# One graph network kernel: the sort pass rewoven, TensorE's loop heads placed, and two orders changed in the edge networks

## The chip, the cores and the metric

One core of one Trainium2 chip runs the whole program. The metric is the time of one execution in microseconds (us), as the device takes it. Three runs of the kernel before took 17660.53, 17686.4 and 17701.15 us, so the median is 17686.4 us.

## The reference, cut to what matters

There are 12500 nodes with 16 features and 412500 edges, sorted by target. Four graph layers follow each other, each behind a layer norm and a relu, each added to the node state `x`:

```python
m = einsum('ei,ej,ijh->eh', h[dst], edge_attr, W_msg_tp) * norm
agg = segment_sum(silu(m) @ W_msg_lin, src)              # layer 0: sums by source
msg = einsum('ea,aoi,ei->eo', edge_attr, W, h[src])      # layer 1: sums by target
e = ln(mlp(edge_attr)); n = ln(mlp(h))                   # layer 2: encoders
for s in range(2):                                       # and two edge networks
    e = e + ln(mlp(concat(e, n[src], n[dst])))
    n = n + ln(mlp(concat(n, segment_sum(e, dst))))
out = gcn(relu(gcn(h, W1, b1)), W2, b2)                  # layer 3: two weighted convolutions
```

The MLPs have 64 hidden units and a silu. `mlp` and `ln` are per edge or per node.

## The kernel before, in words

The edges are cut into 104 blocks (`BLOCKS`) of 3968 edges, 128 partitions with 31 each. The first edge pass computes layer 0's messages and at the same time brings the edges of each block into an order by source ("sort pass", `sorted_message`, line 622). All later edge passes read what it stored: a convolution (`sorted_conv`), the first edge network with the edge encoder, the second edge network (both are `sorted_mlp`, line 1755, with `enc` true and false), and two gcn passes. Node passes lie between them.

Each pass is one program per engine. `in_pairs` (line 88) writes out the first six blocks and then a loop over pairs of blocks, 49 turns of two bodies each, and a few bodies that drain the pipeline. The order in `body` is the order in which an engine issues its instructions; engines meet through semaphores alone. `Chain.at("step", k)` is the count that a semaphore has when that step of block k is done.

**Sort pass.** In one body an engine works on three blocks. *Places* of block k: VectorE (DVE) turns edge ends into a cell, a one-hot matrix `hot_c` (L889), eight pieces of a one-hot matrix of targets `hot_d` (L894), then ranks (L896 to L920) and, after a matmul on TensorE (PE, L1133), the place of each edge (L923 to L944). PE counts (L1121) and turns each piece of `hot_d` (L1130) into PSUM, and ScalarE (ACT) copies it out (L1051). *Messages* of block k-1: PE multiplies each turned piece with a window of the node table (L1144), DVE multiplies the result by the edge attributes (L956, `prod`), sums it (L962) and ACT applies the silu (L1064). Then GpSimd (POOL) writes the 3968 records to their places with 31 indirect DMAs (L828), which wait for the index (L950) and for the silu. *Sums* of block k-3: SyncE (SP) loads the sorted slots back (L781), DVE makes three masked copies (L980 to L985) and four pieces of a one-hot matrix `hot` (L992), PE sums with them in float32 (L1165), ACT writes an 8-bit one-hot matrix of targets (L1082 to L1086) and the sums (L1092), POOL adds a spill (L842). In the kernel before each engine does all of places, then all of messages, then all of sums. SP issues, per body, the edge ends of k (L752 to L754), attributes, window and cleared records, the stores of k-4, and last the slots of k-2, once the 31 DMAs of that block have landed.

**Edge networks.** A block has five groups of cells. PE gathers node states by one-hot matmuls (L2404, L2411), then come a hidden layer (L2430 or L2433), an output layer `out1` (L2444), a layer norm on DVE and ACT, and the sums by target. In the first network PE also runs the edge encoder (L2349 to L2369), turns normed states (`first_` L2379, `second_` L2388), sums in float32 (L2471), and ends each body with `carry` (L2475): the carried sum of the block before and 35 matmuls of one column that count the edges. In the second network the states come from DRAM, DVE splits the normed state into three bfloat16 parts (`less0` L2034, `part2` L2038), and PE sums them (`part_sums`, L2458 and L2460).

A branch hint names the loop's back edge ahead of time. Every loop has it as the first instruction of a turn; only PE's loop of the first edge network has it between the two bodies (`hint_between`).

## Time and profile before

| | us |
|---|---|
| median of three runs | 17686.4 |
| the profiled execution | 17701.2 |
| its span, first to last instruction | 17699.5 |
| PE busy in the span | 13912.2 |
| DVE busy | 13068.0 |
| ACT busy | 7125.3 |
| POOL busy | 4621.6 |

A profile is one execution. A group of instructions is a line of the kernel, an engine and an operation with the tiles it writes and reads; "idle before" is the time in which the engine stood still just before it, with what ended that time. In a timeline a row is one instruction, or several of one line in succession (x8), with its start, its length and, in brackets, the idle time before it. "issue" is idle time in which the engine waited for nothing that the profile shows. PEclk is the granted TensorE clock as a share of 2.4 GHz. Matmuls of float32 are counted twice.

### The profile page before, as it was taken

The page shows a single profiled execution, that of the slowest core. Times are in us where ns is not written, and L with a number is a line of the kernel's source. Part 1 is how long each engine was busy: PE and PEld are TensorE (multiplying, and loading weights), DVE is VectorE, ACT ScalarE, POOL GpSimd, SP SyncE. Part 2 cuts the span into 40 slices and gives each one's busy share as a digit, 9 for nine tenths or more (in the row PEclk, how much of TensorE's full clock was granted, in tenths as well). Part 3 has the DMA queues.
Part 4 walks back from the last instruction along what each step waited for, and adds up shares of the span by engine and source line. Part 5 has one row for each costly group of instructions (what it writes and reads, how often), then busy time and mean ns, then how long its engine had stood idle before and what let it go on. Part 6 is the DMA issues. An engine that isn't in the chain of part 4 may idle for free. (4 is left out here: it accounts for less than half of the span.)

```text
span 17699.5 us, 504368 instructions
## 1 busy us (share of the span) xinstructions
PE 13912.2 (79%) x180289; PEld 12124.8 (69%) x180600; DVE 13068.0 (74%) x30392; ACT 7125.3 (40%) x15316; POOL 4621.6 (26%) x4403
## 2 busy tenths in 40 slices
PE   1677776777767997799999999996799999856565
PEld 0566666666654997588888888885577777646565
DVE  2888888888866997566656656665677777779899
ACT  0454454544542332344444444443344444411111
POOL 0677777777760110011111111110000000001111
PEclk9666666666656998899999999997899999967676
DMA  1122222222222553344444444442444444437566
GB/s 60 54 57 59 57 60 58 57 59 57 60 54 76 157 156 99 96 116 123 117 118 119 118 119 119 121 118 75 131 151 154 154 152 150 132 92 210 167 210 177
DMA packets 1347419, 1956.45 MB, mean 111 GB/s; under 512 B 705453, under 2 KB 923253, under 8 KB 1306317
## 3 DMA queue, kind: packets, MB, share of 16 engines
q1 hardware_dynamic: 1046674, 1621.50, 29.5%
q0 software_dynamic: 209664, 186.01, 7.5%
q10 hardware_dynamic: 90300, 137.10, 2.1%
q8 instruction: 666, 10.91, 0.3%
q14 instruction: 115, 0.93, 0.0%
HBM read 1443.57 MB, written 501.97 MB: 110 GB/s over the span
## 5 line engine op out<-in xcount | busy, mean ns | idle before, releaser
L828 POOL DMA_INDIRECT records<-e_sort_rec,e_sort_index x3224 | 3295.8, 1022 | 1347.4 <-issue 920.3
L2411 PEld LDWEIGHTS e_s_ps_h<-e_s_pick,e_s_parts 128*64 128x64 bf16 x61776 | 1965.7, 113 | 298.7 <-issue 137.0
L2411 PE MATMUL e_s_ps_h<-e_s_pick,e_s_parts 128*64 128x128 bf16 x61776 | 2028.9, 223 | 108.7 <-issue 108.7
L1165 PE MATMUL e_sort_acc<-e_sort_thirds,e_sort_hot 128*128 128x48 f32 x6864 | 1488.8, 414 | 301.4 <-DVE e_sort_hot L992 301.4
L1165 PEld LDWEIGHTS e_sort_acc<-e_sort_thirds,e_sort_hot 128*128 128x128 f32 x6864 | 1472.1, 332 | 332.1 <-DVE e_sort_hot L992 332.1
L2530 POOL DMA_DIRECT2D states<-e_s_second_t x520 | 480.3, 924 | 4176.9 <-ACT e_s_second_t L2259 4108.3
L2006 DVE TENSOR_SCALAR e_s_pick<-e_s_rows,lane_below 128x1024 bf16<-128x1024 bf16 (+1 forms) x3120 | 1179.1, 434 | 372.2 <-PE e_s_ps_h L2411 350.7
L2046 DVE TENSOR_TENSOR e_s_unit<-e_s_ps_o,lane_out 128x512 f32<-128x512 f32 (+1 forms) x520 | 324.9, 625 | 1421.0 <-PE e_s_ps_o L2369 1420.7
L2521 POOL DMA_INDIRECT e_s_spill<-send,e_s_lists x208 | 218.3, 1049 | 3633.1 <-PE e_s_ps_h L2433 2741.9
L1082 ACT ACTIVATE e_sort_away<-iota,e_sort_slots 128x128 f32<-128x128 f32 x3640 | 1107.5, 388 | 10.1
L2444 PE MATMUL e_s_ps_o<-w_eblk,e_s_act 128*128 128x128 f32 x7488 | 1015.1, 276 | 98.2 <-DVE e_s_unit L2055 81.6
L2444 PEld LDWEIGHTS e_s_ps_o<-w_eblk,e_s_act 128*128 128x128 f32 x7488 | 949.6, 191 | 147.9 <-DVE e_s_unit L2055 101.4
L1144 PE MATMUL e_sort_y<-e_sort_window,e_sort_turned 128*128 128x128 f32 x6448 | 988.1, 323 | 19.9 <-DVE e_sort_prod L956 19.9
L1144 PEld LDWEIGHTS e_sort_y<-e_sort_window,e_sort_turned 128*128 128x128 f32 x6448 | 942.2, 232 | 53.2 <-DVE e_sort_prod L956 30.0
L2232 ACT ACTIVATE e_s_act<-e_s_ps_h,col_eenc 128x512 f32<-128x512 f32 (+1 forms) x520 | 335.4, 645 | 1525.0 <-PE e_s_ps_h L2360 1525.0
L2471 PE MATMUL e_s_ps_sum<-e_s_unit,e_s_wide 128*128 128x128 f32 x7280 | 899.0, 275 | 0.1
L2404 PE MATMUL e_s_ps_h<-e_s_to_hot,e_s_window 128*64 128x512 bf16 (+2 forms) x6240 | 824.0, 367 | 90.9 <-DVE e_s_to_hot L2007 78.2
L1130 PE MATMUL e_sort_turn<-ident,e_sort_hot_d 128*128 128x128 bf16 x3224 | 491.6, 306 | 506.0 <-ACT e_sort_turned L1051 498.8
L1419 PE MATMUL e_s_g<-e_s_parts,e_s_pick 128*128 128x48 bf16 x20592 | 773.5, 206 | 119.8 <-DVE e_s_pick_own L1315 63.7
L2266 ACT ACTIVATE e_s_act<-e_s_ps_h,col_state 128x512 f32<-128x512 f32 (+1 forms) x1040 | 663.9, 638 | 502.5 <-PE e_s_ps_h L2430 256.2
L2471 PEld LDWEIGHTS e_s_ps_sum<-e_s_unit,e_s_wide 128*128 128x128 f32 x7280 | 854.9, 192 | 0.7 <-issue 0.7
L1419 PEld LDWEIGHTS e_s_g<-e_s_parts,e_s_pick 128*128 128x128 bf16 x20592 | 750.5, 112 | 138.1 <-issue 70.2
(558 smaller groups left out, 31254.5 us busy)
## 6 DMA issues: line engine op xcount, KB each, us to landing
e_s_rows<-rows_d SPq DMA_DIRECT2D x312, 1088.0 KB, 5.3
e_s_hot<-hots_d SPq DMA_DIRECT2D x520, 560.0 KB, 3.9
e_s_to_rows<-rows_d SPq DMA_DIRECT2D x208, 608.0 KB, 5.9
e_s_rows<-rows_d SPq DMA_DIRECT2D x208, 544.0 KB, 4.4
e_s_rows<-rows_d SPq DMA_DIRECT2D x208, 512.0 KB, 5.2
e_s_to_rows<-rows_d SPq DMA_DIRECT2D x208, 512.0 KB, 6.2
states<-e_s_first_t ACTq DMA_DIRECT2D x416, 256.0 KB, 2.1
states<-e_s_second_t POOLq DMA_DIRECT2D x416, 256.0 KB, 4.2
```

The source lines that it names most:

```text
L828: pool.indirect_dma_start(records, bass.IndirectOffsetOnAxis(ap=index[x][:, t:t + 1], axis=0), rec[x][:, t, :], None,).then_inc(written[x] ...
L1082: last = act.activation(away[:, n - c, :], iota128[:, :], ACT.Square, scale=-1.0, bias=slots[x][:, n, 1:2])
L1130: mm = pe.matmul(ps_turn[:, (n - t) * LANES:(n - t + 1) * LANES], hot_d[:, n, :], ident16[:, :], start=True, stop=True)
L1144: mm = pe.matmul(ps_y[j % 2][0:LANES, (n - t) * AF:(n - t + 1) * AF], turned[x][:, n, :], window[x][:, :], start=True, stop=True)
L1165: mm = pe.matmul(acc[sum_bank(c)][:, sum_at(c)], hot[:, c, :], thirds[:, c, :, :].rearrange("p h f -> p (h f)"), start=False, stop=last an ...
L1419: mm = pe.matmul(ps_g[g][:, at:at + 3 * F], pick[x][:, h, c * LANES:(c + 1) * LANES], parts[:, SPAN * c + h, :, :].rearrange("p r f -> p ( ...
L2006: dve.tensor_scalar(pick[p][:, h, 0:(f - c) * LANES], rows_[:, c * LANES:f * LANES], lane_below[:, h:h + 1], None, ALU.is_equal).then_inc( ...
L2266: act.activation(act1[p][:, 0:turned(s)], hidden_bank(x, s)[:, 0:turned(s)], ACT.Silu, bias=(col_state if enc else col_state1)[:, :]).then ...
L2404: pe.matmul(halves[half][:, 0:n_ * LANES], window[:, r, 1, :], to_pairs[:, half, 0:n_, :], start=r == 0, stop=False, skip_group_check=True)
L2411: mm = pe.matmul(halves[half][:, j * LANES:(j + 1) * LANES], parts[:, SPAN * c + h, r, :], pick[p][:, h, (c - c0) * LANES:(c - c0 + 1) * L ...
L2444: mm = pe.matmul(ps_o1[p % NB][:, j * LANES:(j + 1) * LANES], act1[p][:, j * LANES:(j + 1) * LANES], W[f"eblk1{rnd}"][:, :], start=enc, st ...
L2471: mm = pe.matmul(ps_sum[:, 0:2 * D if enc else D], wide[s][:, (c - c0) * LANES:(c - c0 + 1) * LANES], units_of(x, c), start=c == 0, stop=F ...
```

## The change

It has four parts.

1. Sort pass: on DVE, ACT and PE the three blocks of a body are woven together. A turn of eight pieces holds, per piece, one `hot_d` and one turn of block k, one message matmul group and one `prod` of block k-1, and pieces of DVE's sums of block k-3; the ranks and places of block k come last on DVE. ACT copies records first, and the silu stands between the second and third group of 8-bit targets. On PE the matmul that the places wait for follows the sums. The third piece of `hot` reads the constant from SBUF (`iota128`) instead of PSUM.
2. PE's loops in all passes start at the first instruction slot of a fetch block (`head_slot`), and the hint of PE's first edge network loop moves to the loop's head like all others.
3. First edge network, PE: `carry` goes ahead of the last group of `out1`.
4. Second edge network, DVE: the first picks and the windows of the next block go from the body's end to its fifth group, ahead of `less0` of the fourth group.

```diff
-def in_pairs(eng, n, delay, body, hint_between=False):
+def in_pairs(eng, n, delay, body):
...
+    at_block = {eng.engine: 0} if eng.engine == mybir.EngineType.PE else None
+    with eng.bass.Fori(3, n // 2, engines=[eng.engine], hint_back_edge=True, head_slot=at_block) as j:
+        body(j * 2, 0, 6)
+        body(j * 2 + 1, 1, 6)
...
 # sort pass, DVE
-                    if inside(k):
-                        place(k, x, before)
-                    if before >= 1 and (not isinstance(k, int) or k - 1 < BLOCKS):
-                        message(k - 1, y, before - 1)
-                    if before >= 3:
-                        sum_(k - 3, y, before - 3)
+                    if new:
+                        cells_(k, x, before)
+                    if sent:
+                        indices(k - 1, y, before - 1)
+                    for j in range(len(TURNS)):
+                        if new:
+                            target_hot(k, x, j, before)
+                        if sent:
+                            products(k - 1, y, j, before - 1)
+                        if summed_ and j == 1:
+                            thirds_low(k - 3, y, before - 3)
+                        if summed_ and j == 2:
+                            thirds_top(k - 3, y, before - 3)
+                        if summed_ and j == 3:
+                            thirds_rest(k - 3, y, before - 3)
+                        if summed_ and j in (4, 5, 6):
+                            sum_hot(k - 3, y, j - 4, before - 3)
+                    if sent:
+                        message(k - 1, y, before - 1)
+                    if summed_:
+                        sum_hot(k - 3, y, 3, before - 3)
+                        spill_rows(k - 3, y, before - 3)
+                    if new:
+                        ranks(k, x, before)
+                        places(k, x, before)
...
+                    numbers = iota128[:, :] if g in (1, 2) else ps_iota
+                    if g == 3:
+                        dve.wait_ge(bt.sem, bt.at("early", k))
...
 # sort pass, ACT
+                    if sent:
+                        message(k - 1, y, before - 1)
+                    if new:
                         place(k, x, before)
-                    if before >= 1 and (not isinstance(k, int) or k - 1 < BLOCKS):
-                        message(k - 1, y, before - 1)
-                    if before >= 3:
+                    if summed_:
                         sum_(k - 3, y, before - 3)
+                        targets(k - 3, y, 0, before - 3)
+                        targets(k - 3, y, 1, before - 3)
+                    if sent:
+                        silu_(k - 1, y, before - 1)
+                    if summed_:
+                        targets(k - 3, y, 2, before - 3)
+                        targets(k - 3, y, 3, before - 3)
+                        sums(k - 3, y, before - 3)
...
 # sort pass, PE
+                    for j in range(len(TURNS)):
+                        if sent:
+                            message(k - 1, y, j, before - 1)
+                        if new and j == 0:
+                            count(k, x, before)
+                        if new:
+                            turn(k, x, j, before)
+                    if summed_:
                         sum_(k - 3, y, before - 3, isinstance(k, int) and k == BLOCKS + 2)
+                    if new:
+                        spills(k, x, before)
+                    if summed_:
+                        sum_spills(k - 3, y, before - 3)
...
 # second edge network, DVE
+                    if inside(k) and s == NG - 1:
+                        picks(k, x, 0, before)
+                        windows(k, x, before)
                     if not enc and out_ and s >= 1:
                         less0(k - 2, x, s - 1, before - 2)
...
-                if inside(k):
-                    windows(k, x, before)
-                if inside(k):
-                    picks(k, x, 0, before)
                 if not enc and out_:
                     part2(k - 2, x, 4)
...
 # edge networks, PE
+                    if enc and out_ and s == NG + 1:
+                        carry(k - 2, x, before - 2)
                     if main and 2 <= s < NG + 2:
                         out1(k - 1, y, s - 2, before - 1)
-                if enc and out_:
-                    carry(k - 2, x, before - 2)
-
-            in_pairs(pe, BLOCKS, 2, body, hint_between=enc)
+
+            in_pairs(pe, BLOCKS, 2, body)
```

## Rows read from the trace of the kernel before

**Rows 1.** Stretches: sort pass, first edge network; engines' busy us, PEclk, DMA, GB/s

```profile
455.00:5280.00 4825.00, 3357.18 (x20994) 3027.89 (x20992) 3981.92 (x8042) 2366.87 (x6439) 3463.24 (x3328) 0.61 0.21 58
...
7265.00:12075.00 4810.00, 4573.28 (x61351) 3989.03 (x61353) 2914.53 (x7113) 2261.25 (x3917) 579.53 (x612) 0.97 0.48 119
```

The five busy times are those of PE, PE's weight loads (PEld), DVE, ACT and POOL.

**Rows 2.** Timeline of POOL, one block of the sort pass

```profile
2999.36 0.97 POOL L828 DMA_INDIRECT records<-e_sort_rec,e_sort_index  x1 [3.49 <-ACT e_sort_rec L1064]
...
3003.31 1.74 POOL L828 DMA_INDIRECT records<-e_sort_rec,e_sort_index  x1 [0.30 <-issue]
...
3040.94 1.61 POOL L842 DMA_INDIRECT agg<-e_sort_merged,e_sort_spill_at  x1 [0.30 <-issue]
3045.63 0.97 POOL L828 DMA_INDIRECT records<-e_sort_rec,e_sort_index  x1 [3.08 <-ACT e_sort_rec L1064]
```

**Rows 3.** Groups by line, 3000 to 4000 us: POOL's record writes (busy, mean ns | idle)

```profile
L828 POOL DMA_INDIRECT records<-e_sort_rec,e_sort_index x676 | 692.1, 1024 | 272.0 <-issue 192.8 <-ACT e_sort_rec L1064 72.8 <-DVE e_sort_index L950 6.4
```

**Rows 4.** Timeline of DVE, one block of the sort pass

```profile
3002.87 1.35 DVE L992 TENSOR_TENSOR e_sort_hot<-e_sort_lower,iota 128x1152 f32<-128x1152 f32 x1
...
3016.44 1.15 DVE L896 TENSOR_TENSOR e_sort_pair<-e_sort_cell 128x961 f32<-128x961 f32 x1
...
3029.51 0.19 DVE L923 TENSOR_TENSOR e_sort_spill_rank<-e_sort_within,e_sort_misc 128x31 f32<-128x31 f32 x1 [3.69 <-PE e_sort_misc L1133]
...
3031.85 0.18 DVE L950 CAST e_sort_index<-e_sort_place 128x31 int32<-128x31 f32 x1
...
3039.84 4.29 DVE L962 TENSOR_REDUCE e_sort_summed<-e_sort_prod 128x496 f32<-128x3968 f32 x1
```

**Rows 5.** Timeline of PE and ACT, sort pass: sums, messages, one target group

```profile
3003.01 14.31 PE L1165 MATMUL e_sort_acc<-e_sort_thirds,e_sort_hot 128*128 128x48 f32 x66 [2.90 <-DVE e_sort_hot L992]
...
3075.61 3.39 PE L1144 MATMUL e_sort_y<-e_sort_window,e_sort_turned 128*128 128x128 f32 x16
...
3000.43 2.73 ACT L1082 ACTIVATE e_sort_away<-iota,e_sort_slots 128x128 f32<-128x128 f32 x9
```

**Rows 6.** Timeline of SP's queue: slots of one block, edge ends after it

```profile
3042.28 0.35 SPq L781 DMA_DIRECT2D e_sort_slots<-records  x1
...
3045.55 0.39 SPq L754 DMA_DIRECT2D e_sort_first<-firsts_d  x1
```

**Rows 7.** Waits of PE, first edge network: total us, times, longest

```profile
PE e_s_ps_h L2411 <- issue: 107.0, 48, 3.5
PE e_s_ps_o L2444 <- DVE e_s_unit L2055: 80.8, 103, 0.9
PE e_s_ps_h L2349 <- issue: 42.0, 48, 1.2
```

**Rows 8.** Timeline of PE, first edge network: inside a turn, then across a turn's end

```profile
9039.92 0.60 PE L2379 MATMUL e_s_ps_u<-ident,e_s_unit 128*128 128x128 f32 x4
...
9078.74 1.02 PE L2479 MATMUL e_s_ps_sum<-ones_lane,e_s_hot 128*128 128x1 bf16 x35
...
9084.89 1.91 PE L2411 MATMUL e_s_ps_h<-e_s_pick,e_s_parts 128*64 128x128 bf16 x49 [2.44 <-issue]
...
9088.60 0.97 PE L2379 MATMUL e_s_ps_u<-ident,e_s_unit 128*128 128x128 f32 x4
```

**Rows 9.** Timeline of DVE, first edge network: the norms that these turns of state wait for

```profile
9037.33 0.69 DVE L2014 TENSOR_TENSOR e_s_unit<-e_s_unit,e_s_stat 128x512 f32<-128x512 f32 x1
...
9083.34 0.69 DVE L2014 TENSOR_TENSOR e_s_unit<-e_s_unit,e_s_stat 128x512 f32<-128x512 f32 x1 [0.42 <-DVE e_s_stat L582]
```

**Rows 10.** Waits of PE, second edge network: total us, times, longest

```profile
PE e_s_ps_sum L2458 <- DVE e_s_split L2038: 136.6, 103, 1.4
```

**Rows 11.** Timeline of DVE and ACT, second edge network: tail of a body

```profile
14050.70 0.69 DVE L2034 TENSOR_TENSOR e_s_less<-e_s_unit,e_s_split 128x512 f32<-128x512 f32 x1 [4.22 <-ACT e_s_split L2292]
...
14058.11 0.35 DVE L2038 TENSOR_TENSOR e_s_split<-e_s_less,e_s_split 128x192 bf16<-128x192 f32 x1
...
14056.95 0.35 ACT L2296 ACTIVATE e_s_split<-e_s_less 128x192 bf16<-128x192 f32 x1
```

More of the change, by code:

```diff
@@ L856, in _, with cells_ @@
             def _(dve):
-                def place(k, x, before):
+                def cells_(k, x, before):
                     src_, dst_ = srcE[x][:, :], dstE[x][:, :]
@@ L920, in place, with places @@
                     dve.tensor_reduce(within[:, :], pair[:, :, :], axis=AX.X, op=ALU.add).then_inc(av.sem, 1)
+                def places(k, x, before):
                     dve.wait_ge(av.sem, av.at("sooner_sum", k))
@@ L944, in place, with indices @@
                     dve.tensor_scalar(base_[:, :], base_[:, :], float(SLOTS), None, ALU.add).then_inc(av.sem, 1)
-                def message(k, x, before):
+                def indices(k, x, before):
                     if before >= 2:
@@ L1075, in sum_, with targets, sums @@
                     act.activation(rows_t[x][:, :], ps_rows, ACT.Copy).then_inc(bs.sem, 1)
[L1076 to L1087 removed]
+                def targets(k, x, g, before):
+                    c, e = HOTS[g]
+                    if g:
+                        act.wait_ge(bs.sem, bs.at(f"target{g - 1}", k))
+                    elif before:
+                        act.wait_ge(bs.sem, bs.end(k - 1))
+                    for n in range(c, e):
+                        last = act.activation(away[:, n - c, :], iota128[:, :], ACT.Square, scale=-1.0, bias=slots[x][:, n, 1:2])
+                    last.then_inc(bs.sem, 1)
+                    act.wait_ge(bs.sem, bs.at(f"away{g}", k))
+                    act.activation(ready_[:, :], lane[:, 0:1], ACT.Copy).then_inc(bs.sem, 1)
+                    act.activation(targets_[x][:, c * LANES // 2:e * LANES // 2].bitcast(FP8), away[:, 0:e - c, :].rearrange("p c l -> p (c l)"), ACT.Relu,
+                                   scale=-1.0, bias=1.0, saturate=False).then_inc(bs.sem, 1)
+                def sums(k, x, before):
                     act.wait_ge(bt.sem, bt.at("merged", k))
@@ L1115, in _, with count @@
             def _(pe):
-                def place(k, x, before):
+                def count(k, x, before):
                     pe.wait_ge(av.sem, av.at("hot_c", k))
@@ L1132, in place, with spills, message @@
+                def spills(k, x, before):
                     pe.wait_ge(av.sem, av.at("lates16", k))
                     pe.matmul(ps_lates, earlier16[:, :], lates16[:, :], start=True, stop=True).then_inc(at_.sem, 1)
-                def message(k, x, before):
-                    pe.wait_ge(attrs_in[x], attrs_of(k, x))
-                    pe.wait_ge(as_.sem, as_.end(k))
-                    for j, (t, e) in enumerate(TURNS):
-                        if j >= 2:
-                            pe.wait_ge(cv.sem, cv.at(f"prod{j - 2}", k))
-                        elif before:
-                            pe.wait_ge(cv.sem, cv.at(f"prod{len(TURNS) - 2 + j}", k - 1))
-                        for n in range(t, e):
-                            mm = pe.matmul(ps_y[j % 2][0:LANES, (n - t) * AF:(n - t + 1) * AF], turned[x][:, n, :], window[x][:, :],
-                                           start=True, stop=True)
-                        mm.then_inc(ct.sem, 1)
+                def message(k, x, j, before):
+                    t, e = TURNS[j]
+                    if j == 0:
+                        pe.wait_ge(attrs_in[x], attrs_of(k, x))
+                        pe.wait_ge(as_.sem, as_.end(k))
+                    if j >= 2:
+                        pe.wait_ge(cv.sem, cv.at(f"prod{j - 2}", k))
+                    elif before:
+                        pe.wait_ge(cv.sem, cv.at(f"prod{len(TURNS) - 2 + j}", k - 1))
+                    for n in range(t, e):
+                        mm = pe.matmul(ps_y[j % 2][0:LANES, (n - t) * AF:(n - t + 1) * AF], turned[x][:, n, :], window[x][:, :],
+                                       start=True, stop=True)
+                    mm.then_inc(ct.sem, 1)
```

111 lines of the change are left out of this document (45 added, 66 removed).

## The prediction, made before the changed kernel ran

> **What bounds the kernel now.** I read the busy times by stretch first, then for each changed pass the waits of the engine that is nearest to its limit, then a timeline of one block. The sort pass takes 4825 us, 46.4 us for each of 104 blocks, and no engine is full in it: DVE works 3981.92 us, 38.3 a block, PE 32.3, and PE's clock is granted at 0.61 on average [rows 1]. What turns over without a pause is POOL: the first write of a block starts at 2999.36, the spill behind the 31st ends at 3040.94 + 1.61 = 3042.55, and the next block begins at 3045.63, after 3.08 us of waiting for ACT's silu [rows 2]. So POOL's own work is 43.2 of 46.3 us. Over 1000 us the waits for the silu add up to 72.8 us, while the 192.8 us put down to "issue" are the 0.3 us between two writes and stay [rows 3]. The silu is late because DVE does all of the places first, stands still 3.69 us for a matmul queued behind PE's sums, and then only multiplies and reduces [rows 4].
>
> The first edge network is PE's: 4573 us busy of 4810, clock 0.97 [rows 1]. Its idle time has three parts, 107.0, 80.8 and 42.0 us [rows 7]. The first comes once a turn of the loop (48 times), in the first gather, 32 recorded matmuls behind the loop's head, and lasts 2.44 us in the turn shown [rows 8]. The third comes at the loop's end itself, also 48 times. The second is the last output layer waiting for DVE.
>
> In the second edge network PE waits 136.6 us, 1.33 a block, for the last `part2` of a block [rows 10]. DVE does it at 14058.11, though ACT had its input done at 14056.95 + 0.35 = 14057.30: windows and picks stand between. Earlier in the same body DVE stands still 4.22 us [rows 11].
>
> **The change, part by part.**
>
> *Sort pass, gain.* If POOL never waits for the silu, 7.28% of 4825 us goes: 351 us. Of that, one ordinary gap of 0.30 us a block stays [rows 2], 104 x 0.30 = 31 us, so 320 us is the most.
>
> *Sort pass, what is added.* The third piece of `hot` now reads its constant from SBUF, as the second does. The write that starts at 3003.31, while the SBUF piece runs (3002.87 to 4.22), takes 1.74 us, against 0.97 undisturbed: 0.77 more [rows 2, 4]. One more such meeting a block costs 104 x 0.77 = 80 us. It may miss the write's sensitive part and cost nothing, or meet two writes and cost 160; I take one meeting, as the row shows. The Trainium skill, "SBUF — State Buffer", section "Who interferes with whom", says that a DVE instruction with two SBUF inputs and a GpSimd instruction that reads SBUF exclude each other for the whole instruction, the later one blocked; that speaks against this edit, and by it the write would wait to 3004.22, 0.91 us instead of the measured 0.77, and the sum would be 95 instead of 80. Net of the sort pass: 320 - 80 = 240 us, 44.0 us a block.
>
> *Does anything else bind at 44.0?* DVE has 38.3 us of work [rows 1]. Its 3.69 us wait goes if PE's matmul for the places comes no later than the ranks. By hand, with PE at its half clock: 16 message records took 3.39 us [rows 5], so 62 take 13.1; with turns and count the eight rounds take PE about 18 us, within DVE's eight rounds, which carry the sums' pieces too. DVE's ranks and places run from 3016.44 to 3031.85, less 3.69 of waiting 11.7 us [rows 4]; they now come last, so the reduce ends at most 38.3 - 11.7 = 26.6 us into the body, some 0.7 later for the first rounds' wait. PE's sums then take 14.31 us from about 23.5 to 37.8, about when DVE's ranks are through, so that wait almost vanishes. ACT does two target groups (9 squares in 2.73 us [rows 5], about 4.1 with the rest) before the silu, which comes near 33 us; the body ends near 40.5. The bound from POOL's side: the last write of a block ends at 3040.64, SP issues the slots at 3042.28 and the last edge end at 3045.55 [rows 6], so with the landing a body can start about 7 us behind that write. POOL needs this body's silu one block and a spill later, 44.0 + 2.2 us behind the write. So the silu may come 39 us into the body: 6 us to spare. What is late next is POOL itself.
>
> *Moved steps on the queues.* SP's order is unchanged; its waits for sums and targets of k-4 are met earlier than the slots' wait, which still comes last. ACT's record copies now come ahead of its eight PSUM copies, under 2 us, while PE is still counting: nothing.
>
> *First edge network.* With `carry` (some 1.05 us, [rows 8]) ahead of the last output group, PE works where it stood: 80.8 us. With the loop's head on a block's first slot, the next block boundary lies 256 instructions away instead of a few dozen, so the following code has time to arrive: 107.0 us. The turn's end keeps perhaps half of its 42.0. That is 209 us from waits alone. Behind the stall the matmuls also run slowly (the `first_` at 9088.60 takes 0.97 us, the one at 9039.92 takes 0.60, the half and the full of 2.4 GHz [rows 8]), so more can come back. The upper bound is DVE: `first_` cannot start before the norm, which ends at 9038.02 and 9084.03, and starts 1.90 and 4.57 us later than that [rows 8, 9]; 6.47 us a turn x 49 turns = 317 us. Above that the norm's wait takes over. I take 250, nearer the waits, since the clock may still fall behind `carry`'s one-column matmuls.
>
> *Second edge network.* The moved picks and windows (2.7 us) go into the 4.22 us of standing. They need rows, lists and the last gather of the block before, all there by then. `part2` can start 14058.11 - 14057.30 = 0.8 us earlier, less 0.05 for the signal: 0.75 x 104 = 78 us; the remaining 0.57 us is ACT's.
>
> *Loop heads elsewhere.* No wait of PE in the other loops comes once a turn under "issue"; I cost them at 0, with 20 us either way for the jumps into the six loops and a worse or better boundary.
>
> **Sum.** 240 + 250 + 78 = 568 us off 17701.2 us, that is 17133. The profiled execution is 14.8 us above the median of 17686.4, so against the runs I say 17120 us.
>
> **The rivals.**
>
> *A. The stall at the fetch boundary stays* (the change doesn't do what it says: the head is not what makes it). Then the first edge network gives `carry`'s 80.8 less about 10 for the norm: 70. 240 + 70 + 78 = 388, 17298 us. For it: one row of one turn doesn't show a block's boundary. Against: the stall comes at the same place 48 times.
>
> *B. The hint at the head is spent before the turn's end*, 92 us later, and the jump pays a full fetch. Between the end of `carry` (9079.76) and the end of the stall (9084.89) lie 5.1 us [rows 8], the nearest price of a fetch. Less the 0.87 now paid, 49 x 4.2 = 207 us come back: 240 + 43 + 78 = 361, 17325 us. For it: this loop alone had its hint in the middle. Against: the second network's loop has the hint at its head, and the longest wait of PE there is the one for DVE [rows 10]. The Trainium skill, "Runtime: NRT & Kernel Launch", section "Instruction fetch mechanics", says that a taken branch to code outside the resident window must fetch before it goes on; by it B is what happens wherever the loop is longer than the window.
>
> *C. The weave is DVE's or PE's bound after all*, by stalls of some 5 us a body: POOL gets half of its waits back, the sort pass gives 120: 17238 us.
>
> *D. Slower: the eight rounds run in series.* If every round's `prod` waits for that round's message and turn on PE (1.7 + 0.45 us), 8 x 2.15 = 17.2 us come on top of DVE's 38.3: 55.5 a body, 9.2 more than now, 957 us against 328 won elsewhere: 18315 us. It decides from 49.5 us a body on. Against: the message of a round belongs to the block before, whose pieces were turned a body ago, and has two PSUM banks, so PE runs a round ahead.
>
> **How the numbers follow.** The sum as above 0.57, A 0.13, B 0.12, C 0.12, D 0.06; of C, 0.02 is a weave bad enough to leave nothing. The likeliest case's own range goes from 320 + 317 + 78 + 20 = 735 off (16951) to 160 + 209 + 60 - 20 = 409 off (17277). The range 17000 to 17400 holds A, B and C too. A measurement of this kernel tells 0.2% (35 us) from no change. Faster 0.92, same 0.02, slower 0.06.
>
> **What would show it.** Right: POOL's waits for the silu all but gone and writes following at 44 us a block; DVE's L923 waiting under 0.5 us; no PE idle above 1 us in the first network's L2411; `first_` waiting for DVE's L2014; L2458 waiting about 0.6 us. Wrong: POOL still waiting for L1064 over 1 us a block (C or D), "issue" at the loop's head above 2 us (B), or in L2411 (A).

## The result, and the profile after the change

The changed kernel takes 16981.52 us (median of 4 runs, 16973.91 to 16985.81), against 17683.37 us before (4 runs, 17660.53 to 17701.15): 0.9601 times the time before, with a 95% interval of 0.9585 to 0.9616. That is 702 us less; 563 to 566 were forecast, and 16981.5 lies 18.5 us below the range given. Line numbers from here on are the changed kernel's (or the experiment's) and differ from those of the kernel before.

Where the time went is read best by stage. The sort pass is measured from TensorE's first matmul in it to its last; each other stage from the first to the last matmul of one line of TensorE's (in the kernel before L2369 and L2433 for the two edge networks, L1710 for the convolution, L1433 for the two gcn passes):

| stage | before | after | difference | forecast |
|---|---|---|---|---|
| sort pass | 4859.9 us | 4479.0 us | -380.9 | -240 |
| first edge network | 4800.7 | 4538.8 | -261.9 | -250 |
| second edge network | 2912.8 | 2835.9 | -76.9 | -78 |
| convolution, both gcn passes | 1249.9, 1811.5 | 1250.0, 1809.7 | -1.7 | 0 |

These are the two profiled executions, which lie 727 us apart: that of the kernel before was the slowest of its four runs, that of the changed kernel the fastest. A stage of unchanged code differs by up to some 20 us between traces (the first edge network as it was takes 4779.6 us in the trace of `before_sbuf_piece`, the changed sort pass 4478 to 4494 in the seven traces that have it). With that in mind two stages came out as forecast, and the sort pass gave 141 us more. It goes first. The busy times of the two stretches in the changed kernel (columns as in [rows 1]; the stretch of the sort pass is 4444 us instead of 4825):

```profile
455.00:4899.00 4444.00, 3269.47 (x20938) 3038.85 (x20938) 3904.48 (x8040) 2340.94 (x6434) 3394.88 (x3328) 0.64 0.22 63
6884.00:11427.00 4543.00, 4456.15 (x61285) 3895.83 (x61285) 2900.95 (x7105) 2246.26 (x3907) 577.98 (x611) 1.00 0.50 125
```

POOL's own groups over the whole sort pass, record writes and spills, of the kernel before (busy, mean ns of one | idle before them and its causes):

```profile
L828 POOL DMA_INDIRECT records<-e_sort_rec,e_sort_index x3224 | 3295.8, 1022 | 1347.4 <-issue 920.3 <-ACT e_sort_rec L1064 396.6 <-DVE e_sort_index L950 29.9
L842 POOL DMA_INDIRECT agg<-e_sort_merged,e_sort_spill_at x104 | 167.4, 1610 | 55.2 <-issue 31.1 <-ACT e_sort_merged L1092 19.8 <-DMA agg<-e_sort_merged,e_sort_spill_at 4.4
```

and of the changed kernel:

```profile
L815 POOL DMA_INDIRECT records<-e_sort_rec,e_sort_index x3224 | 3220.4, 999 | 1034.6 <-issue 954.7 <-ACT e_sort_rec L1090 51.9 <-ACT e_sort_rec L1094 14.0
L829 POOL DMA_INDIRECT agg<-e_sort_merged,e_sort_spill_at x104 | 174.5, 1678 | 55.3 <-issue 31.1 <-ACT e_sort_merged L1126 19.8 <-DMA agg<-e_sort_merged,e_sort_spill_at 4.5
```

These four lines split the 381 us. POOL's idle time in front of the record writes fell by 1347.4 - 1034.6 = 313 us, where 320 were forecast. The wait for the silu went from 396.6 to 14.0; of the 396.6, 64.7 were the first block's, which now waits 51.9 for ACT's copy (L1090), and what is left in front of each block's first write, the 14.0 too, is the ordinary gap of 0.3 us. The spills cost 7 us more. And the record writes themselves became shorter, 1022 to 999 ns, which is 75 us less, where the sum had put 80 us **more** for the third piece of `hot` that now reads SBUF. So the wrong term is the collision, and it was wrong by 155 us.

The waits of DVE from 3000 to 4000 us (total, times, longest) show the rest of the chain as forecast, and that the order has turned round: DVE now waits for the edge ends, which SP fetches behind POOL's writes, so POOL sets the pace at 42.4 us a block.

```profile
DVE e_sort_prod L952 <- PE e_sort_y L1192: 37.9, 24, 1.6
DVE e_sort_dlo L852 <- DMA e_sort_first<-firsts_d: 31.8, 19, 3.3
DVE e_sort_spill_rank L916 <- PE e_sort_misc L1180: 5.2, 11, 0.5
```

The 3.69 us wait of [rows 4] is at most 0.5 us here. The waits of PE in the first edge network, which answer to [rows 7], are now

```profile
PE e_s_ps_u L2435 <- DVE e_s_unit L2073: 75.7, 102, 1.1
PE e_s_ps_o L2425 <- DVE e_s_unit L2105: 4.7, 2, 4.3
PE e_s_ps_o L2500 <- DVE e_s_unit L2114: 0.9, 1, 0.9
```

The three waits of [rows 7] (107.0, 80.8 and 42.0 us) are gone but for 0.9 us; `first_` (L2435) waits 75.7 us for the norm instead. And PE's busy time fell from 4573 to 4456 us at a clock of 1.00 instead of 0.97. In the second edge network the wait of [rows 10] went from 136.6 to 56.9 us, 0.56 a block where 0.57 were forecast:

```profile
PE e_s_ps_sum L2514 <- DVE e_s_split L2097: 56.9, 102, 0.6
PE e_s_ps_h L2489 <- DMA e_s_states<-states: 41.1, 74, 2.0
```

### The profile page after: what moved, and what is told of

Read it like the earlier page. It is cut to its first block and busy times, and to the rows that moved or that the text cites. A ratio compares the mean times of both kernels' runs of the same rounds, so it can differ in the third digit from the quotient of the medians.

```text
span 16972.2 us, 504685 instructions
## 1 busy us (share of the span) xinstructions
PE 13729.1 (81%) x180600; PEld 12049.9 (71%) x180600; DVE 12985.4 (77%) x30392; ACT 7088.9 (42%) x15316; POOL 4548.4 (27%) x4403
## 5 line engine op out<-in xcount | busy, mean ns | idle before, releaser
L815 POOL DMA_INDIRECT records<-e_sort_rec,e_sort_index x3224 | 3220.4, 999 | 1034.6 <-issue 954.7
L2467 PEld LDWEIGHTS e_s_ps_h<-e_s_pick,e_s_parts 128*64 128x64 bf16 x61776 | 1900.5, 110 | 175.7 <-issue 6.7
L2467 PE MATMUL e_s_ps_h<-e_s_pick,e_s_parts 128*64 128x128 bf16 x61776 | 1954.7, 219 | 5.5 <-issue 5.5
L1212 PE MATMUL e_sort_acc<-e_sort_thirds,e_sort_hot 128*128 128x48 f32 x6864 | 1448.7, 407 | 6.0 <-DVE e_sort_hot L995 6.0
L1079 ACT ACTIVATE e_sort_turned<-e_sort_turn 128x512 f32<-128x512 f32 x832 | 485.9, 584 | 1950.3 <-PE e_sort_turn L1175 1950.3
L1192 PE MATMUL e_sort_y<-e_sort_window,e_sort_turned 128*128 128x128 f32 x6448 | 1229.8, 350 | 2.1 <-DVE e_sort_prod L952 2.0
L1192 PEld LDWEIGHTS e_sort_y<-e_sort_window,e_sort_turned 128*128 128x128 f32 x6448 | 1100.6, 256 | 3.1 <-DVE e_sort_prod L952 2.9
L1175 PE MATMUL e_sort_turn<-ident,e_sort_hot_d 128*128 128x128 bf16 x3224 | 402.6, 261 | 569.2 <-DVE e_sort_hot_d L883 562.0
```

What stands on the lines that cost most here:

```text
L815: pool.indirect_dma_start(records, bass.IndirectOffsetOnAxis(ap=index[x][:, t:t + 1], axis=0), rec[x][:, t, :], None,).then_inc(written[x] ...
L1079: act.activation(turned[x][:, t:e, :].rearrange("p t q -> p (t q)"), ps_turn[:, 0:(e - t) * LANES], ACT.Copy).then_inc(as_.sem, 1)
L1192: mm = pe.matmul(ps_y[j % 2][0:LANES, (n - t) * AF:(n - t + 1) * AF], turned[x][:, n, :], window[x][:, :], start=True, stop=True)
L1212: mm = pe.matmul(acc[sum_bank(c)][:, sum_at(c)], hot[:, c, :], thirds[:, c, :, :].rearrange("p h f -> p (h f)"), start=False, stop=last an ...
L2467: mm = pe.matmul(halves[half][:, j * LANES:(j + 1) * LANES], parts[:, SPAN * c + h, r, :], pick[p][:, h, (c - c0) * LANES:(c - c0 + 1) * L ...
```

## The experiments

### Which DVE instruction lengthens a record write

Two theories were set against each other: the price of the prediction (0.77 us for each piece of `hot` that reads SBUF) and a phase theory, by which it matters where in a write the piece falls. Four kernels change the number of such pieces.

**One: the kernel before, with the third piece alone reading SBUF.**

```
-    numbers = iota128[:, :] if g == 1 else ps_iota
-    if g == 2:
+    numbers = iota128[:, :] if g in (1, 2) else ps_iota
+    if g == 3:
         dve.wait_ge(bt.sem, bt.at("early", k))
```

> The kernel before, with one edit of the change alone: the third piece of hot reads its constant from SBUF. Price theory (the prediction's): one more lengthened record write a block, 0.77 us x 104 = 80 us, so 1.0045 times the kernel before. Phase theory: a record write is lengthened only when a DVE instruction with two SBUF inputs starts while that write is under way; in the kernel before the third piece starts 1.25 us into a write that the second piece has already stretched to 1.74 us, behind its sensitive part, and ends 0.6 us into the next. So no more than the one write is long: 0 us, 1.000 times, within 16 us either way.

Measured: 17673.21 us, 1.0003 times the kernel before (0.9993 to 1.0012). The price falls as a price for each piece. One block: first the two pieces on DVE, back to back, then the writes on POOL.

```profile
2998.80 2.62 DVE L992 TENSOR_TENSOR e_sort_hot<-e_sort_lower,iota 128x1152 f32<-128x1152 f32 x2
```

```profile
2999.24 1.75 POOL L828 DMA_INDIRECT records<-e_sort_rec,e_sort_index  x1 [0.30 <-issue]
3001.29 0.96 POOL L828 DMA_INDIRECT records<-e_sort_rec,e_sort_index  x1 [0.30 <-issue]
```

Still one long write. The group of all 3224 writes is even 19 us shorter than before, because the writes stand a little differently against the ranks.

**Two: the changed kernel with the third piece on PSUM again,** behind the summed reduce.

```
-    numbers = iota128[:, :] if g in (1, 2) else ps_iota
-    if g == 3:
+    numbers = iota128[:, :] if g == 1 else ps_iota
+    if g == 2:
...
-    if summed_ and j in (4, 5, 6):
+    if summed_ and j in (4, 5):
...
+        sum_hot(k - 3, y, 2, before - 3)
         sum_hot(k - 3, y, 3, before - 3)
```

> The changed kernel with its third piece of hot reading PSUM again; for that it stands behind the summed reduce, with the wait for PE's first sums ahead of it. Price theory: 80 us less than the changed kernel in the sort pass, 16900 us. Phase theory: in the changed kernel this piece starts 0.01 us ahead of a write (3029.59 against 3029.60) and that write takes 0.95 us, so there is nothing to win: 0 us, with some 20 us either way because the ranks now stand at another phase of the writes; 16980 us.

Measured: 17002.12 us, 0.9624 (0.9608 to 0.964). The piece gone, the pass is not shorter: 4488.0 us, 9 more, which lies within the 4478 to 4494 of the seven traces of the unchanged pass. A price of 80 us is excluded.

**Three: no piece on SBUF.** As above, with `numbers = ps_iota` for all, the wait at `g == 1`, and pieces 1 to 3 behind the reduce.

> The changed kernel with no piece of hot reading its constant from SBUF; the last three stand behind the summed reduce and the wait for PE's first sums. Price theory: 2 x 80 = 160 us less, 16820 us. Phase theory: only the second piece meets a write (1.56 against 0.96 us), 0.6 to 0.7 us x 104 = 65 to 73 us less, 16910 us, again with some 20 us either way from the ranks. A third possibility: DVE, whose reduce and ranks now wait for PE's sums, becomes late for the slots or the silu, and POOL waits over 0.5 us a block: no gain or a loss.

Measured: 16931.44 us (16926.62 to 16945.77), 0.9584 (0.9568 to 0.96); sort pass 4430.7 us, 48 less than in the changed kernel, against 65 to 73 of the phase theory and 160 of the price.

**Four: all pieces on SBUF.** `numbers = iota128[:, :]`, and no wait for PE's sums.

> The changed kernel with all four pieces of hot reading their constant from SBUF, at their old places. Price theory: 2 x 80 = 160 us more, 17140 us. Phase theory: the first piece starts 0.73 us into a write and stretches it by about 0.7 us; by that the writes behind it come 0.7 us later, so that the second piece starts at a write's start and stretches none; the fourth starts 0.4 us into a write and adds some 0.1. Still one long write a block: 0 to 15 us more, 16980 to 17000 us.

Measured: 17088.17 us, 0.9673 (0.9657 to 0.9689), 107 more than the changed kernel: both theories missed, the phase theory (0 to 15) the more. The groups of the writes in the four kernels, in that order:

```profile
L828 POOL DMA_INDIRECT records<-e_sort_rec,e_sort_index x3224 | 3277.0, 1016 | 1363.0 <-issue 920.0 <-ACT e_sort_rec L1064 411.7 <-DVE e_sort_index L950 30.1
```

```profile
L815 POOL DMA_INDIRECT records<-e_sort_rec,e_sort_index x3224 | 3234.5, 1003 | 1035.4 <-issue 961.9 <-ACT e_sort_rec L1091 52.8 <-ACT e_sort_rec L1095 18.6
```

```profile
L815 POOL DMA_INDIRECT records<-e_sort_rec,e_sort_index x3224 | 3165.5, 982 | 1035.6 <-issue 974.2 <-ACT e_sort_rec L1092 51.9 <-DVE e_sort_prod L952 8.2
```

```profile
L815 POOL DMA_INDIRECT records<-e_sort_rec,e_sort_index x3224 | 3332.6, 1034 | 1033.8 <-issue 962.4 <-ACT e_sort_rec L1088 51.9 <-ACT e_sort_rec L1092 11.3
```

Idle time hardly moves between the last three; the writes' mean length is what differs, 1003, 982 and 1034 ns. So the idea of a phase was right, but I had it the wrong way round. The changed kernel's own timeline shows the right one. DVE:

```profile
3027.13 1.34 DVE L995 TENSOR_TENSOR e_sort_hot<-e_sort_lower,iota 128x1152 f32<-128x1152 f32 x1
...
3029.59 1.40 DVE L995 TENSOR_TENSOR e_sort_hot<-e_sort_lower,iota 128x1152 f32<-128x1152 f32 x1
...
3038.90 1.15 DVE L887 TENSOR_TENSOR e_sort_pair<-e_sort_cell 128x961 f32<-128x961 f32 x1
```

and POOL:

```profile
3026.48 0.96 POOL L815 DMA_INDIRECT records<-e_sort_rec,e_sort_index  x1 [0.30 <-issue]
3027.74 1.56 POOL L815 DMA_INDIRECT records<-e_sort_rec,e_sort_index  x1 [0.30 <-issue]
3029.60 0.95 POOL L815 DMA_INDIRECT records<-e_sort_rec,e_sort_index  x1 [0.30 <-issue]
...
3038.44 0.96 POOL L815 DMA_INDIRECT records<-e_sort_rec,e_sort_index  x1 [0.31 <-issue]
3039.70 1.18 POOL L815 DMA_INDIRECT records<-e_sort_rec,e_sort_index  x1 [0.30 <-issue]
```

The first piece starts 0.65 us into the write of 3026.48, and that one keeps its 0.96 us. The next write, at 3027.74, starts while the piece is running, finds 3028.47 - 3027.74 = 0.73 us of it left, and is 0.60 longer. At 3039.70 the write finds 0.35 us of the first `pair` product left and is 0.22 longer. **A write that starts while a DVE instruction with two SBUF inputs is running is longer by what is left of that instruction, less 0.13 us.** One that is already under way when the instruction starts is not touched. The second piece (3029.59) and its write (3029.60) start together, and the write goes free.

The eight different sort passes traced here (the rows of the table below) hold 2474 writes that started at least 0.06 us behind such an instruction's start with more than 0.15 us of it left; their excess over 0.96 us differs from (rest - 0.128 us) by 0.001 us in the mean, with a standard deviation of 0.012. The 2219 with 0.128 us or less left are 0.001 us longer in the mean. Between 0.01 and 0.04 us behind its start it is one or the other: the write goes free or waits for the whole instruction. Where a piece of `hot` is that close ahead of a write and the write goes free, the piece takes 1.41 us in the mean (293 of them, as the 1.40 at 3029.59); where the write waits, the piece keeps its 1.35 (83 of them). What the writes lose, summed over the pass by the instruction that was running at their start, in us:

```
                      hot pieces   first pair   late pair   thirds   masked    all
kernel before               79.5         40.9        61.6     17.6      0.0   200.8
changed kernel              77.0         21.6         1.9     27.7      0.5   125.3
before, third on SBUF       79.9         51.1        31.6     17.2      0.0   182.0
third piece on PSUM         66.3         52.7         1.9     22.9      0.4   139.5
no piece on SBUF             0.0          1.3        17.6     29.3     18.4    70.5
all pieces on SBUF         179.2          5.7        19.4     29.0      0.8   237.6
ranks 0.4 us later          81.7         60.3         2.5     26.2      0.8   167.0
ranks 1.0 us later          80.9          0.5         1.0     56.1     -0.2   136.0
```

(The columns are L995's pieces that read `iota`, the `pair` products L887, L908 and L890, and the products for `thirds`, L980 to L988; of the 200.8, about 1 us has no such instruction beside it; writes with none beside them can be a shade under 0.96 us, so a row's parts can exceed its total.) So the added piece cost next to nothing: of the 77.0 the second piece has 70.9 and the third 6.2, since it starts so close ahead of a write (6 to 14 in the seven traces of the unchanged pass). And the change gave 79 us back in the `pair` products, of which the prediction said nothing. The late product now runs beside the spill and ends as the next write starts:

```profile
3003.37 1.15 DVE L908 TENSOR_TENSOR e_sort_pair<-e_sort_late,e_sort_sooner 128x961 f32<-128x961 f32 x1
```

```profile
3002.60 1.61 POOL L829 DMA_INDIRECT agg<-e_sort_merged,e_sort_spill_at  x1 [0.30 <-issue]
3004.52 0.97 POOL L815 DMA_INDIRECT records<-e_sort_rec,e_sort_index  x1 [0.30 <-issue]
```

The table's own spread is small: the seven traces of the unchanged pass lose 125 to 136 us in all.

With all pieces on SBUF the phase theory had the first meeting right in size, and the later ones wrong: by the rule a piece that a write follows by 0.02 us or so may hold it for 1.2 us. The four pieces cost 69, 56, 39 and 15 us over the pass.

### A test of that rule

The rule was then used to forecast two kernels that move DVE's ranks against the writes, by an idle reduce ahead of them.

```
 def ranks(k, x, before):
+    dve.tensor_reduce(within[:, 0:10], sooner[:, 0:10, :], axis=AX.X, op=ALU.add).then_inc(av.sem, 1)
```

> The changed kernel with an idle reduce of 310 elements (one SBUF input) ahead of DVE's ranks in the sort pass, which moves them some 0.39 us later. Rule read from the five traces so far: a record write that starts while a DVE instruction with two SBUF inputs is running is longer by what is left of that instruction less 0.13 us; one that is already under way when the instruction starts is not. In the changed kernel the first pair product runs from 3038.90 to 3040.05 and the write at 3039.70 finds 0.35 us left and is 0.22 us longer. By the rule it will find 0.74 us left: 0.61 us longer, 0.39 us x 104 = 41 us more, 17020 us. Rival (DVE's extra work is what counts): DVE waits 1.7 us a block for the edge ends, so 0.4 us more work costs nothing: 16980 us.

Measured: 17028.63 us, 0.963 (0.9614 to 0.9646), 47 us more than the changed kernel, against 41; the sort pass takes 4518.8 us, 40 more, and the first product now costs its writes 60.3 us instead of 21.6. The rival, by which DVE's added work costs nothing, is out. With `0:29` for `0:10`:

> The same with an idle reduce of 899 elements, some 1.0 us. By the rule: the first pair product now starts 0.2 us behind the start of the write at 3039.70 and ends 0.09 us into the next one, so neither is longer; the later products meet none either: 0.22 us x 104 = 23 us less than the changed kernel though DVE does 1 us more a block, 16960 us. Rival (extra work on DVE costs in proportion, or a meeting costs by its count): the same as the changed kernel or up to 104 us more.

Measured: 16987.38 us, 0.9604 (0.9588 to 0.962): the same as the changed kernel, 6 us more and not 23 less. Half of the forecast holds, and a block shows it:

```profile
3044.42 1.15 DVE L888 TENSOR_TENSOR e_sort_pair<-e_sort_cell 128x961 f32<-128x961 f32 x1
3045.60 1.16 DVE L891 TENSOR_TENSOR e_sort_pair<-e_sort_pair,e_sort_sooner 128x961 f32<-128x961 f32 x1
```

```profile
3044.22 0.96 POOL L815 DMA_INDIRECT records<-e_sort_rec,e_sort_index  x1 [0.30 <-issue]
3045.48 0.95 POOL L815 DMA_INDIRECT records<-e_sort_rec,e_sort_index  x1 [0.30 <-issue]
```

The product falls between two writes' starts, and its 21.6 us are gone, as forecast. But the writes of the next block then meet `thirds` at another phase and lose 56.1 us there instead of 27.7. A meeting that is taken away moves every later one.

### The first edge network: head, counts, hint

Three kernels undo or shift one part, one undoes both, and one moves the hint.

```
-    with eng.bass.Fori(3, n // 2, engines=[eng.engine], hint_back_edge=True, head_slot=at_block) as j:
+    with eng.bass.Fori(3, n // 2, engines=[eng.engine], hint_back_edge=True) as j:
```

> The changed kernel without the placing of TensorE's loop heads (all six loops; the hint stays at the head, the counts ahead of the last output layer). Theory of the prediction: the head's place is what took away the 107.0 us of stalls in the first gather and half of the 42.0 at the loop's end, so the first edge network takes 128 us more, up to 170 with the clock lost behind the stalls: 17110 to 17150 us, and the other stages 0 within 20 us. Rival 1: the hint in the middle was the cause, and a hint at the head is enough: 0, 16980 us. Rival 2: without a placed head the hint at the head is spent at the turn's end, 4 to 5 us a turn x 49 on top: over 17300 us.

Measured: 17078.48 us, 0.9669 (0.9652 to 0.9685); the first edge network takes 4620.2 us, 81 more, and the other stages within 9 us of the changed kernel. PE's waits there:

```profile
PE e_s_ps_h L2466 <- issue: 98.2, 78, 2.9
PE e_s_ps_u L2434 <- DVE e_s_unit L2072: 34.9, 54, 0.9
PE e_s_ps_h L2415 <- issue: 9.4, 14, 2.0
```

The stalls are back, 98.2 us in the gather (L2466) and 14.0 elsewhere, 112 in all, so the head's place is what removes them; but 41 us of them only take the place of the wait for the norm (75.7 to 34.9). With `{eng.engine: 200}` for `{eng.engine: 0}`:

> The changed kernel with TensorE's loop heads 200 instructions behind a block's start instead of on it. Theory of distance: what matters is how many instructions lie between the head and the next block boundary, now 56 instead of 256, so the first edge network stalls once a turn some 25 recorded matmuls behind the head, as the kernel before did at 32: 100 to 170 us more, 17080 to 17150 us. Rival: only that the head is fixed matters, or the hint: 0, 16980 us.

Measured: 17086.81 us, 0.9671 (0.9655 to 0.9687); the network takes 4641.4 us.

```profile
PE e_s_ps_h L2467 <- issue: 118.2, 84, 2.3
PE e_s_ps_u L2435 <- DVE e_s_unit L2073: 34.8, 54, 0.8
```

A fixed head is not enough: 200 instructions further on, the gather stalls 118.2 us. One turn shows where:

```profile
9019.52 0.55 PE L2405 MATMUL e_s_ps_h<-ident,e_s_lists 128*128 128x128 f32 x3
9020.00 0.84 PE L2460 MATMUL e_s_ps_h<-e_s_to_hot,e_s_window 128*64 128x512 bf16 x6
...
9023.00 1.75 PE L2467 MATMUL e_s_ps_h<-e_s_pick,e_s_parts 128*64 128x128 bf16 x56 [1.72 <-issue]
...
9030.02 0.78 PE L2467 MATMUL e_s_ps_h<-e_s_pick,e_s_parts 128*64 128x128 bf16 x21 [1.52 <-issue]
```

The first stall has 56 of the gather's 72 matmuls behind it, so it stands 3 + 6 + 16 = 25 recorded matmuls behind the head, in each of the loop's 48 jumps, as the theory of distance said. Without a placed head 49 are behind it, 32 from the head, again 48 times, as in [rows 8]. In both kernels a second, shorter stall often follows in the next gather (33 and 30 times), 125 recorded matmuls later (56 + 8 + 4 + 6 + 51 here); each has its weight load, so that is 250 instructions and a few waits. The Trainium skill, "Runtime: NRT & Kernel Launch", section "Instruction fetch mechanics", gives blocks of 256 instructions, and the two stalls agree with that.

```
-    if enc and out_ and s == NG + 1:
-        carry(k - 2, x, before - 2)
     if main and 2 <= s < NG + 2:
         out1(k - 1, y, s - 2, before - 1)
+if enc and out_:
+    carry(k - 2, x, before - 2)
```

> The changed kernel with the counts (carry) behind the last output group again. Theory of the prediction: out1 waits 0.78 us a block for DVE again, 80.8 us more in the first edge network, 17060 us. Rival: with the stalls gone PE reaches the last group later against DVE than before, and the wait is mostly gone anyway: 0 to 40 us, 16980 to 17020 us.

Measured: 17016.68 us, 0.9628 (0.9612 to 0.9645); the network takes 4572.7 us, 34 more, as the rival had it.

```profile
PE e_s_ps_o L2500 <- DVE e_s_unit L2114: 80.0, 102, 0.9
PE e_s_ps_h L2405 <- issue: 13.2, 49, 0.3
...
PE e_s_ps_u L2435 <- DVE e_s_unit L2073: 0.8, 1, 0.8
```

The wait for DVE is back with its full 80.0 us, and the one for the norm is gone instead: a PE that has waited for the last layer comes late enough for the norm. So `carry` moves PE's waits more than it removes them: they differ by some 17 us in all. PE is also busy 21 us longer, at a clock of 0.99. One turn, and a stretch of it (columns as in [rows 1]), show why:

```profile
9263.35 1.02 PE L2535 MATMUL e_s_ps_sum<-ones_lane,e_s_hot 128*128 128x1 bf16 x35
9264.64 0.90 PE L2405 MATMUL e_s_ps_h<-ident,e_s_lists 128*128 128x128 f32 x3 [0.27 <-issue]
```

```profile
9264.60:9267.00 2.40, 2.36 (x15) 1.21 (x17) 2.10 (x9) 0.73 (x3) 0.01 (x1) 0.50 0.65 79
```

Behind the counts the granted clock fell to 0.50 though the stall there was only 0.27 us. Past the stage's first 15 us this happened 16 times, each time within 1 us of the end of the counts; in the changed kernel it never did. Both together undone (hint still at the head):

> The changed kernel with both parts of the first edge network's change undone, but for the branch hint, which stays at the loop's head: no placed head, and the counts behind the last output group. If the two parts add up (81 us and 34 us when undone singly), PE's first edge network takes 4539 + 81 + 34 = 4654 us at a granted clock of 0.99 to 1.00; 17095 us. Rival 1: stall and one-column matmuls together cost PE its clock (0.97 in the kernel before): near the 4801 us of the kernel before, 17240 us. Which of the two tells whether the missing 147 us belong to the hint's place (then they are not lost here) or to the pair.

Measured: 17221.01 us, 0.9737 (0.9721 to 0.9753); the network takes 4770.3 us. Singly the two cost 81 and 34 us, together 231: rival 1. Of the 116 us beyond the sum, 72 are PE's busy time and the rest waits, the one at the loop's head above all (L2404): 43.0 us here, 4.6 in `no_head_slot` and 13.2 in `carry_at_end`. PE at a turn's end:

```profile
9066.05 1.02 PE L2534 MATMUL e_s_ps_sum<-ones_lane,e_s_hot 128*128 128x1 bf16 x35
9068.08 0.54 PE L2404 MATMUL e_s_ps_h<-ident,e_s_lists 128*128 128x128 f32 x3 [1.01 <-issue]
...
9072.18 2.88 PE L2466 MATMUL e_s_ps_h<-e_s_pick,e_s_parts 128*64 128x128 bf16 x49 [0.98 <-issue]
```

and stretches of the same time (columns as in [rows 1]):

```profile
9065.00:9067.50 2.50, 1.74 (x41) 1.65 (x41) 2.50 (x7) 1.50 (x5) 1.71 (x2) 1.00 0.48 56
9067.50:9072.00 4.50, 3.12 (x32) 2.02 (x32) 3.71 (x14) 0.60 (x3) 0.00 (x0) 0.63 0.83 220
9072.00:9075.00 3.00, 2.82 (x50) 2.65 (x50) 1.54 (x6) 0.00 (x0) 0.00 (x0) 0.50 0.59 231
```

The granted clock is 1.00 while the 35 one-column matmuls run, and falls to 0.50, that is 1.2 of 2.4 GHz, behind them and the idle 1.01 us (past the stage's first 15 us it falls 53 times here, and twice in `no_head_slot`); the gather's 49 matmuls take 2.88 us where they take 1.58 in the kernel that has the stall but not the counts at that place. Over the network PE is busy 4556.6 us at a clock of 0.97, against 4463.5 at 1.00 there. With the counts at the end the 0.78 us wait for DVE stands just ahead of them too; which of the two the clock answers to was not tried apart. Last, the hint:

```
+            body(j * 2, 0, 6)
+            hint = eng.mark_branch_hint_location()
+            body(j * 2 + 1, 1, 6)
...
-            in_pairs(pe, BLOCKS, 2, body)
+            in_pairs(pe, BLOCKS, 2, body, hint_between=enc)
```

> The changed kernel with the hint of the first edge network's loop in its middle again and no placed heads; the counts stay ahead of the last output group. If the hint's place is what the missing 147 us hang on: 4620 + 100 to 147 = 4720 to 4770 us for this network against 4620 with the hint at the head, 17180 to 17230 us. If it is not: 4620 us, 17078 us.

Measured: 17084.63 us, 0.9662 (0.9646 to 0.9679); the network takes 4634.3 us, 14 more than with the hint at the head, and no head placed in either. With the counts ahead of the last layer, then, the hint's place is not the cause; with the counts at the end it was not tried, and the 4770.3 us of the kernel with both undone lie 9 to 30 us below the two traces of the network as it was.

### The second edge network

```
-    if inside(k) and s == NG - 1:
-        picks(k, x, 0, before)
-        windows(k, x, before)
...
+if inside(k):
+    windows(k, x, before)
+if inside(k):
+    picks(k, x, 0, before)
```

> The changed kernel with windows and picks of the second edge network at the tail of DVE's body again. Theory of the prediction: part2 comes 0.75 us later in each of 104 blocks, 78 us more, all of it in the second edge network; 17060 us. Rival: the 77 us came from the placed loop head, not from DVE's order: 0, 16980 us.

Measured: 17077.98 us, 0.9667 (0.9651 to 0.9683); this network takes 2924.9 us, 89 more.

```profile
PE e_s_ps_sum L2517 <- DVE e_s_split L2097: 135.9, 102, 1.4
```

The wait is back at 135.9 us, 79 more, with a placed head: it is DVE's order. The other 10 us were not followed up.

## Why the prediction was wrong in the sort pass and right elsewhere

**The step that failed** is the one headed "sort pass, what is added": one more meeting a block at 0.77 us, 80 us, to take off the gain. The pass changed by 313 us of idle time, as the step before it said (320), and by 75 us of shorter writes, where that step had 80 us of longer ones. It failed twice. It had allowed for a cost of nothing, but not for a gain. It priced the added instruction by the one that was there, though its cost hangs on which write starts while it runs; and it looked at the added one only, though the reordering moved all the other instructions with two SBUF inputs against the writes. The late `pair` product alone had cost 61.6 us and costs 1.9 now. The gain was capped at "320 us is the most", since only the waits counted as something to lose; but each of the 3224 writes had 0.062 us on top of its 0.96 before, 201 us in all.

The price itself was measured well: 0.77 by the row, 0.906 - 0.128 = 0.778 by the rule. The Trainium skill, "SBUF — State Buffer", section "Who interferes with whom", has a DVE instruction with two SBUF inputs and a GpSimd instruction that reads SBUF shut each other out, the later one blocked for the whole of the earlier. The traces agree for a write that comes later, but for 0.13 us. A DVE instruction that comes well into a write is not held by it: the piece at 3027.13 starts 0.65 us into one and takes its ordinary 1.34 us. Where both start together and the write goes free, the piece is 0.06 us longer (1.41 against 1.35), so there the write does hold it, for far less than its 0.96 us. A write that reads SBUF only for a moment near its start would fit both; no run here shows when it reads.

**Does anything else bind?** As forecast: the reduce ends 26.3 us into DVE's body (26.6 plus 0.7 were said), the silu comes at 32.8 (33), and POOL is what is late next. Rival C is out. Rival D is out too: DVE's rounds wait 1.6 us a block for PE.

**First edge network:** the sum was right, 262 against 250 (241 against the faster of the two traces of the network as it was), but its make-up was not, so that it came out is in part luck. The three waits lost 229 us, with all of the 42.0 at the loop's end where half was taken (the head's place or `carry`'s alone takes most of them, as the 13.2 and 4.6 above show); the wait for the norm took 75 back, which had been put at the upper bound only; and 117 us of busy time went, nearly all with the clock, where the prediction feared that it might still fall behind `carry`. The working had 209 from waits and 41 for the rest. The experiments show when the clock falls: with the counts at the body's end, 16 times with the head placed and 53 times with the stalls back as well, and with them ahead of the last layer not once in the changed kernel and twice with the stalls back. That it is the one-column matmuls, and not the wait for DVE ahead of them, is not shown. Rivals A and B are out: no stall is left in L2467 or at the head.

**Second edge network and heads elsewhere:** 77 against 78, and -1.7 against 0.

The likeliest case's own range, 16951 to 17277, held the time; the range of all cases had been cut to 17000 at its lower end, closer to the middle than the bounds of the terms allowed.

## What to carry to other kernels

Where GpSimd writes through indices without a pause, count which DVE instructions have two SBUF inputs and what is left of each when a write starts; that is the cost, and any reordering changes all of it, so bound it by the sum over the pass, on both sides, and not by the one instruction that is added. Waits that one edit removes can be given back to the next dependency (here 75 of 229 us), and two edits that look independent can share a loss: undo them singly and together. Here the version without a piece on SBUF is the fastest that was run, 16931 us, with all of its runs below all of the changed kernel's and 48 us less in the sort pass, though the intervals of the two ratios overlap.

## What the runs showed of the hardware that was not expected

The length of a record write follows from one number, to 0.001 us in the mean of 2474 cases: what is left of the DVE instruction with two SBUF inputs at the write's start, less 0.128 us. A write that is already under way is not touched.

PE's stall behind a loop's jump comes a fixed number of instructions behind the head, set by where the head stands: 25 recorded matmuls with the head at slot 200, 32 where it had not been placed. In the gather it costs 118.2 and 98.2 us, and nothing with the head on a block's first slot; why the code is there in time then was not tried apart. And TensorE's granted clock fell from 1.00 to 0.50 behind a 0.78 us wait, 1.02 us of one-column matmuls and 1.01 us of idleness, in 16 places behind such a wait and such matmuls with 0.3 us of idleness or less, but was 1.00 over the network in the kernel that has stalls of up to 2.9 us and no such matmuls close ahead of them.
